# A graph layer and a mixture of experts: sums that end in PSUM in alternating banks, and a new order around expert 1

## The chip, the cores and the metric

The kernel runs on one core of one Trainium2 chip. The metric is the time of one execution on the device in microseconds (us), lower is better. Engines are named as in the profile: PE is TensorE's matrix multiplication, PEld its weight load, DVE is VectorE, ACT is ScalarE, POOL is GpSimd, SP is SyncE.

## What is computed

Two layers over 2048 rows of 256 numbers. The first is a graph layer with a 2048 x 2048 adjacency matrix, the second a feed-forward layer with 8 experts, of which each row takes the one with the highest logit, and a shared expert for all rows.

```python
deg = jnp.maximum((adj != 0).astype(jnp.float32).sum(-1), 1.0)[..., None]
h = layernorm(x)
dinv = rsqrt(deg)
pooled = (dinv * (adj + eye) * dinv) @ h + h
x = x + relu(pooled @ W + b)

xf = layernorm(x)
logits = xf @ gate_w.T                      # 8 experts
wts, idx = top_k(logits, 1); wts = softmax(wts)
h = silu(xf @ w1[e].T) * (xf @ w3[e].T)     # e: the row's expert, 1024 inner columns
y = (h * comb) @ w2[e].T
y = y + gelu(xf @ sw1.T) @ sw2.T            # the shared expert
x = x + y
```

## The kernel before

Every fp32 product is made from high and low parts: ACT rounds a tensor to its high part, DVE or POOL subtracts it from the original for the low part, and PE multiplies high by high, high by low and low by high in fp32r. The 2048 rows are 16 tiles of 128, and four tiles are a quarter (NQ = 4, QT = 4).

**The front.** For each tile t, z = layernorm(x) @ W is computed (`z_tile`), and its high and low parts are kept side by side in `zz`. Beside it the neighbour sums of quarter 0 run. **A quarter q** of neighbour sums (`agg_quarter`) multiplies 16 adjacency tiles (`agg_part`: `a_hi` from ACT, `a_lo` from POOL, line 395) by `zz` into four PSUM banks, one for each of the quarter's four row tiles; the left half of a bank holds the sum with z's high part, the right half that with its low part. `agg_end` adds the identity's share and closes the sums. The adjacency comes in chunks of two tiles into four buffers; SP loads the next one into a buffer when POOL has made its low parts and DVE has counted its nonzeros (`count_chunk`, lines 756 and 759). After the last count, `degrees` (line 1098) sums the counts by a matrix product.

DVE then ends the layer for the quarter: ACT copies the left halves to `agg` in SBUF (line 574), DVE adds the right halves (`sum_halves`, line 812), takes the inverse degree (`inverse_degree`), multiplies by it and adds z + bias (line 821), applies ReLU and adds to `resid` (line 825), both in `finish_gnn`.

**Shared blocks.** The layer norm of quarter q-1, its transposes (`xf_transposes`, into banks 4 and 5, or 0 and 1 in the last quarter) and their high and low parts (`xfT_highs`, `xfT_lows`) are made while quarter q is summed; behind the sums PE runs the gate of quarter q-1 and then `shared`: a row of 16 blocks (32 in the last run, which does quarters 2 and 3), each with `shared_up` (six products, line 1172), a GELU and its high part on ACT, the low part on POOL (line 411), and `shared_down` (four products, lines 1192 and 1194) two blocks later. The order within is written out by hand: a table of places says between which blocks `gate_back` (the gate's result transposed back), `ranks` (each row's rank in its expert) and, in the last run, the transposes, gate and ranks of quarter 3 stand. On ACT, `tanh_of_z` stands behind the first four GELUs of a quarter's blocks; it waits for `z_top_ok`, the last instruction of DVE's `choose`, and `choose` works on what `gate_back` leaves in PSUM. `shared_up` m waits until GELU m-2 has read its bank. POOL scatters a quarter's rows to `sorted_x` by expert, once `place_rows` has their places.

**Steps.** 23 steps of 128 sorted rows follow; with these inputs the experts need 2, 2, 2, 3, 2, 3, 3 and 3 steps by the reference's routing. A step does `up` (24 products, line 1253), a transpose of the next rows, `down` of the step before (lines 1280 and 1281) and `hid_transposes` (line 1266). Expert weights lie in `ering`, which has two slots. Each expert comes twice: as three high parts (1, 3 and 2 thousand columns, `expert_high`, POOL's own DMA queue, line 424), and as 12 raw pieces `eraw` of 512 columns through a ring of four buffers on SP's queue (line 338), from which POOL makes the 12 low parts (`expert`, line 445; DVE makes the first eight of expert 0). Low part 0 needs the first high part, low 2 the second, low 8 the third. A step's `up` waits for the first 8 low parts of its expert, its `down` for all 12. A slot's first two high parts are loaded when the expert in it has begun its last step's transposes (a wait on `xsT_ps` at low 8 of the expert before), the third when that expert's last `down` is done (a wait on `steps_done` at low 4). SP issues the first three row loads of `sorted_x` behind raw piece 11, and stores 16 tiles of `resid` between later raw pieces.

## Time and profile before

| | |
|---|---|
| three runs | 497.62, 493.37, 496.64 us, median 496.64 us |
| profiled execution, its own time | 496.5 us |
| its span, mean granted clock | 494.9 us, 0.976 |
| busy: PE / DVE / ACT / POOL | 91% / 55% / 40% / 67% of the span |
| DMA | 82.61 MB, mean 167 GB/s |

The span runs from the first to the last instruction of the core. A timeline row gives the start, the duration, the engine, the line and what it writes and reads; a bracket at its end gives the idle time of the engine before it and what ended that. "x4" joins four instructions in one row. A clock of 1.00 is 2.4 GHz for TensorE and 0.50 is 1.2 GHz.

### The profile page before, as it was taken

How to read it: one execution, taken by the hardware profiler on the slowest of the kernel's cores; microseconds unless marked ns; L12 is line 12 of the kernel's file. 1: busy time of each engine (PE TensorE's matmuls, PEld its weight loads, DVE VectorE, ACT ScalarE, POOL GpSimd, SP SyncE). 2: the span in 40 equal slices, each digit the busy share in tenths (PEclk: the TensorE clock that was granted, in tenths of full speed). 3: DMA queues.
4: the chain of work that ended last, by engine and by line, in shares of the span. 5: the costliest groups of instructions: out<-in, count | busy, mean ns of one | idle time of the engine just before them, and what ended most of it. 6: DMA issues, size and time to landing. Idle time of an engine off the chain costs nothing.

```text
span 494.9 us, 8933 instructions
## 1 busy us (share of the span) xinstructions
PE 449.6 (91%) x2620; PEld 384.3 (78%) x2621; DVE 272.4 (55%) x543; ACT 198.6 (40%) x435; POOL 333.0 (67%) x309
## 2 busy tenths in 40 slices
PE   5899977899989999889987999799999999999992
PEld 5788755798769887777975888688888888888881
DVE  4998799844687268858763334223343343333331
ACT  3655822564536543584552232222232332332330
POOL 3888857277955797557865675766667777888112
PEclk9999999999999999899999999889999999999997
DMA  7564240501341052369565689888888787455100
GB/s 250 190 210 156 79 149 22 182 1 49 122 153 61 2 176 98 81 225 357 145 199 171 229 280 331 250 315 281 324 279 301 254 307 234 59 70 73 11 1 0
DMA packets 41116, 82.61 MB, mean 167 GB/s; under 512 B 5120, under 2 KB 16768, under 8 KB 39040
## 3 DMA queue, kind: packets, MB, share of 16 engines
q1 hardware_dynamic: 28528, 47.60, 30.2%
q0 software_dynamic: 7536, 29.39, 19.0%
q10 hardware_dynamic: 5024, 5.27, 3.4%
q8 instruction: 15, 0.25, 0.2%
q14 instruction: 13, 0.11, 0.1%
HBM read 74.74 MB, written 8.41 MB: 168 GB/s over the span
## 4 chain that ended last, share of the span: by engine, by line
PE 50%; DVE 12%; POOL 10%; DMA 6%; issue 5%; ACT 3%; POOLq 1%; SPq 1%; DVEq 0%; ACTq 0%
PE bank L1253 20%; PE bank L1172 7%; PE bank L1280 7%; PE bank L1192 5%; DVE count L759 5%; POOL ering L445 4%; DMA eraw<-in_experts 4%; PE bank L1281 3%; POOL a_lo L395 3%; PE bank L1266 3%; DVE rows L735 3%; PE bank L1194 2%; DMA ering<-in_experts 1%; POOL gel_lo L411 1%; PE bank L1080 1%
## 5 line engine op out<-in xcount | busy, mean ns | idle before, releaser
L445 POOL TENSOR_TENSOR ering<-eraw,ering 128x512 fp32r<-128x512 f32 x88 | 111.9, 1307 | 54.2 <-DMA eraw<-in_experts 25.2
L1253 PE MATMUL bank<-ering,xsT_hi 128*128 x368 | 122.4, 404 | 6.1 <-POOL ering L445 3.4
L395 POOL TENSOR_TENSOR a_lo<-araw,a_hi 128x512 fp32r<-128x512 f32 x64 | 92.8, 1467 | 30.6 <-ACT a_hi L539 30.3
L1080 PE MATMUL bank<-zz,a_hi 128*128 128x512 f32 (+1 forms) x256 | 93.4, 405 | 7.1 <-POOL a_lo L395 7.0
L1000 DVE SCALAR_TENSOR_TENSOR hid<-bank,xs,sil 128x512 f32<-128x512 f32 x46 | 34.5, 751 | 98.7 <-ACT sil L663 98.7
L1253 PEld LDWEIGHTS bank<-ering,xsT_hi 128*128 128x128 f32 x368 | 70.4, 191 | 21.7 <-issue 6.6
L1253 PE MATMUL bank<-ering,xsT_lo 128*128 x184 | 72.7, 395 | 0.0
L1082 PE MATMUL bank<-zz,a_lo 128*128 128x256 f32 (+1 forms) x256 | 72.2, 282 | 0.0
L663 ACT ACTIVATE sil<-bank 128x512 f32<-128x512 f32 x46 | 27.5, 599 | 106.0 <-PE bank L1253 106.0
L1280 PE MATMUL bank<-ering,hidT_hi 128*128 x184 | 67.4, 406 | 1.2 <-DVE hidT_lo L1008 1.2
L411 POOL TENSOR_TENSOR gel_lo<-gel,gel_hi 128x256 fp32r<-128x256 f32 x58 | 43.9, 759 | 35.4 <-ACT gel_hi L597 34.5
L1080 PEld LDWEIGHTS bank<-zz,a_hi 128*128 128x128 f32 x256 | 48.7, 190 | 20.3 <-issue 8.6
L504 POOL DMA_INDIRECT out<-y_rows,row_token x23 | 35.9, 1559 | 31.5 <-DVE y_rows L1016 26.4
L539 ACT ACTIVATE a_hi<-araw 128x512 fp32r<-128x512 f32 x64 | 39.7, 628 | 34.7 <-PE bank L1082 23.1
L1192 PE MATMUL bank<-sw_r,gel_hi 128*128 128x512 f32 x128 | 48.9, 403 | 4.6 <-POOL gel_lo L411 3.0
L1281 PE MATMUL bank<-ering,hidT_lo 128*128 x184 | 51.5, 280 | 0.0
L1082 PEld LDWEIGHTS bank<-zz,a_lo 128*128 128x128 f32 x256 | 49.0, 191 | 0.0
L759 DVE SCALAR_TENSOR_TENSOR count<-araw,count 128x1024 bf16<-128x1024 f32 x28 | 45.8, 1635 | 2.8 <-DVE count L759 0.5
L1172 PE MATMUL bank<-xfT_hi,sw_hi 128*128 128x256 f32 x128 | 38.0, 297 | 4.2 <-DVE dinv L806 3.1
L1280 PEld LDWEIGHTS bank<-ering,hidT_hi 128*128 128x128 f32 x184 | 34.6, 188 | 8.6 <-issue 1.4
L1253 PEld LDWEIGHTS bank<-ering,xsT_lo 128*128 128x128 f32 x184 | 35.3, 192 | 7.0
L1172 PE MATMUL bank<-xfT_lo,sw_hi 128*128 128x256 f32 x128 | 36.5, 285 | 0.0
(154 smaller groups left out, 795.4 us busy)
## 6 DMA issues: line engine op xcount, KB each, us to landing
eraw<-in_experts SPq DMA_DIRECT2D x96, 256.0 KB, 5.5
araw<-in_adj_t SPq DMA_DIRECT2D x32, 512.0 KB, 4.7
ering<-in_experts POOLq DMA_DIRECT2D x8, 1536.0 KB, 8.5
ering<-in_experts POOLq DMA_DIRECT2D x8, 1024.0 KB, 7.7
ering<-in_experts POOLq DMA_DIRECT2D x8, 512.0 KB, 4.6
xs<-sorted_x ACTq DMA_DIRECT2D x20, 129.0 KB, 3.8
resid<-in_x SPq DMA_DIRECT2D x4, 512.0 KB, 9.0
sw_raw<-in_sw_t ACTq DMA_DIRECT2D x2, 1024.0 KB, 6.6
```

Of the source, the lines that this page charges most:

```text
L395: pool.tensor_tensor(a_lo[:, u % AR, :], araw[:, u // CJ, u % CJ, :], a_hi[:, u % AR, :].bitcast(F32), ALU.subtract).then_inc(adj_lo_ok, 1)
L411: pool.tensor_tensor(gel_lo[:, u, :], gel[:, u, :], gel_hi[:, u, :].bitcast(F32), ALU.subtract).then_inc(sh_lo, 1)
L445: pool.tensor_tensor(ering[:, slot, 1, c * ECW:(c + 1) * ECW], eraw[:, c % ER, :], ering[:, slot, 0, c * ECW:(c + 1) * ECW].bitcast(F32), ...
L539: act.activation(a_hi[:, u % AR, :], araw[:, u // CJ, u % CJ, :], ACT.Copy).then_inc(adj_hi_ok, 1)
L759: dve.scalar_tensor_tensor(into, araw[:, r, :, :], 0.0, into, ALU.not_equal, ALU.add).then_inc(adj_counted, CJ)
L1080: pe.matmul(acc(it)[:, :], a_hi[:, s, it * P:(it + 1) * P], zt, start=first, stop=False)
L1082: ins = pe.matmul(acc(it)[:, 0:D], a_lo[:, s, it * P:(it + 1) * P], zt[:, 0:D], start=False, stop=False)
L1172: ins = pe.matmul(bank[4 + m % 2][:, 0:HALF], w[:, k, ib * P:(ib + 1) * P], a[:, q % 2, k, half * HALF:(half + 1) * HALF], start=n == 0, s ...
L1192: pe.matmul(shared_bank(hq, k)[:, :], gel_hi[:, m % 2, k * P:(k + 1) * P], sw2_r[:, ib, :, :].rearrange("p h d -> p (h d)"), start=ib == 0 ...
L1253: ins = pe.matmul(bank[2 * w + h][:, :], a[:, k, :], ering[:, bass.ds(slot, 1), part, at:at + BANK].rearrange("p a n -> p (a n)"), start=n ...
L1280: pe.matmul(bank[6][:, :], hidT_hi[:, k, :], w2, start=k == 0, stop=False)
L1281: ins = pe.matmul(bank[6][:, 0:D], hidT_lo[:, k, :], ering[:, bass.ds(slot, 1), 0, W2AT + k * D:W2AT + (k + 1) * D].rearrange("p a n -> p ...
```

## The change

1. *Banks.* The four banks of the neighbour sums alternate: 0 to 3 in quarters 0 and 2, 4 to 7 in quarters 1 and 3. All that uses the other four (`xf_bank`, `gate_bank`, `logit_in`, `rank_in`, `degree_in`, `up_bank`, `shared_bank`) moves with them, with new waits for them.
2. *End of the layer.* `sum_halves` goes. `first_products` computes low half * dinv + (z + bias) in place in PSUM, `finish_gnn` adds high half * dinv to it in PSUM, and the ReLU and the addition to `resid` read PSUM. Twelve instructions per quarter stand where twelve stood.
3. *Order of DVE.* Two of the last four counts stand before `xfT_lows`, the inverse degree before the sums, the gate's copy between the products; in quarters 1 to 3 `choose` follows the end of the layer.
4. *Order of PE.* `degrees` stands before `agg_end`. `gate_back` is at place 6 of the shared blocks (5 in the last run) instead of 2, the ranks at 9 (7) instead of 5 (9). The wait for the last shared addition stands behind the `up` of step 1.
5. *Experts.* Expert 1's low parts wait for expert 0 at low 11 instead of low 8; for later experts the wait for `steps_done` and the third high part's load stand at low 3 instead of 4, and the next expert's first loads at low 9, behind low 8 as before. The three first row loads stand behind raw pieces 13, 14 and 15.

```diff
-    EARLY_RANKS_AT, STD_AT, THIRD_RANKS_AT, XF_AT, GATE_AT, RANKS_AT = 5, 8, 9, 10, 13, 16
+    EARLY_RANKS_AT, STD_AT, THIRD_RANKS_AT, XF_AT, GATE_AT, RANKS_AT = 9, 8, 7, 10, 13, 16
...
+        def acc(q, it):
+            return bank[(4 if q % 2 else 0) + it]
+        def other(q):
+            return 0 if q % 2 else 4
         def xf_bank(q, b):
-            return bank[(0 if q == NQ - 1 else 4) + b]
+            return bank[other(q + 1) + b]
...
                     sp.dma_start(eraw[:, c % ER, :], experts[e, :, c * ECW:(c + 1) * ECW]
                                  ).then_inc(eraw_loaded[c % ER], 16)
-                    if n == EC - 1:
+                    if n == EC + 1:
                         sp.wait_ge(routed, 1)
                         sp.wait_ge(scattered, 16 * NT)
                         sp.wait_ge(filled, 16 * (E + 1))
-                        for i in range(FIRST_ROWS):
+                    if EC + 1 <= n < EC + 1 + FIRST_ROWS:
+                        for i in range(n - EC - 1, n - EC):
...
+            def expert(e, slot, last=None, ahead=None, next_at=EC - 3):
+                for c in range(EC):
+                    static = isinstance(e, int)
+                    if c == EC // 4 and last is not None:
                         pool.wait_ge(steps_done, last)
+                        if static:
+                            low(e, slot, c)
+                        expert_high(e, slot, 2)
+                        if static:
+                            continue
+                    if c == next_at and ahead is not None:
                         pool.wait_ge(xsT_ps, ahead)
+                        if static:
+                            low(e, slot, c)
                         expert_high(e + 1, 1 - slot, 0)
                         expert_high(e + 1, 1 - slot, 1)
+                        if static:
+                            continue
+                    low(e, slot, c)
...
-            expert(1, 1, ahead=end_of(0))
+            expert(1, 1, ahead=end_of(0), next_at=EC - 1)
...
-            def sum_halves(q):
-                for it in range(QT):
-                    dve.wait_ge(agg_copied, q * QT + it + 1)
-                    dve.tensor_tensor(agg[:, it, :], acc(it)[:, D:2 * D], agg[:, it, :], ALU.add
-                                      ).then_inc(agg_free, 1)
-            def finish_gnn(q):
-                dve.wait_ge(agg_free, (q + 1) * QT)
+            def first_products(q):
                 dve.wait_ge(dinv_ok, q + 1)
                 dve.wait_ge(bias_added, (q + 1) * QT)
                 for it, t in enumerate(group(q)):
-                    chained(dve.scalar_tensor_tensor(agg[:, it, :], agg[:, it, :], dinv2[:, it:it + 1],
-                                                     norm[:, t, :], ALU.mult, ALU.add))
+                    dve.wait_ge(agg_copied, q * QT + it + 1)
+                    low = acc(q, it)[:, D:2 * D]
+                    chained(dve.scalar_tensor_tensor(low, low, dinv2[:, it:it + 1], norm[:, t, :], ALU.mult, ALU.add))
+            def finish_gnn(q):
+                settle()
+                for it in range(QT):
+                    low = acc(q, it)[:, D:2 * D]
+                    chained(dve.scalar_tensor_tensor(low, agg[:, it, :], dinv2[:, it:it + 1], low,
+                                                     ALU.mult, ALU.add))
                 settle()
                 for it, t in enumerate(group(q)):
-                    chained(dve.scalar_tensor_tensor(resid[:, t, :], agg[:, it, :], 0.0, resid[:, t, :],
-                                                     ALU.max, ALU.add))
-                settle()
+                    dve.scalar_tensor_tensor(resid[:, t, :], acc(q, it)[:, D:2 * D], 0.0, resid[:, t, :],
+                                             ALU.max, ALU.add).then_inc(agg_free, 1)
+                dve.wait_ge(agg_free, (q + 1) * QT)
...
                 normalize(NQ + q - 1, group(q - 1))
+                count_chunks(q, RAW, NC - 2)
                 xfT_lows(q - 1)
-                count_chunks(q, RAW, NC)
-                sum_halves(q)
+                count_chunks(q, NC - 2, NC)
+                inverse_degree(q)
+                first_products(q)
                 copy_gate(q - 1)
-                inverse_degree(q)
+                finish_gnn(q)
                 logits(q - 1)
                 if q < NQ - 1:
                     choose(q - 1)
-                finish_gnn(q)
-                if q < NQ - 1:
+                    read_ranks(q - 1)
                     place_rows(q - 1)
...
             hids(0, 0)
             rows_low(2, 1)
+            hid_lows(0)
             add_shared(2 * NQ - 1)
-            hid_lows(0)
...
                 for j in range(TURN, NT):
-                    agg_part(j, j % AR, q * NT + j)
+                    agg_part(q, j, j % AR, q * NT + j)
+                pe.wait_ge(xfT_lo_ok, 2 * q)
+                if q > 1:
+                    pe.wait_ge(sh_free, 4 * (q - 1))
+                degrees(q)
                 agg_end(q)
...
             def gate_back(q):
                 pe.wait_ge(gate_copied, q + 1)
+                pe.wait_ge(agg_free, min(q + 2, NQ) * QT)
...
-                degrees(q)
                 if q < NQ - 1:
-                    shared((q - 1) * 2 * NI, 2 * NI, {1: degrees_read(q), 2: lambda: gate_back(q - 1), EARLY_RANKS_AT: lambda: ranks(q - 1)})
+                    shared((q - 1) * 2 * NI, 2 * NI, {6: lambda: gate_back(q - 1), EARLY_RANKS_AT: lambda: ranks(q - 1)})
-            shared(LAST, 4 * NI, {1: degrees_read(NQ - 1), 2: lambda: gate_back(NQ - 2), THIRD_RANKS_AT: lambda: ranks(NQ - 2),
+            shared(LAST, 4 * NI, {5: lambda: gate_back(NQ - 2), THIRD_RANKS_AT: lambda: ranks(NQ - 2),
...
-            pe.wait_ge(sh_free, 2 * 2 * NQ)
             def one_step(s, u, loads):
                 up(s)
+                if u == 1:
+                    pe.wait_ge(sh_free, 2 * 2 * NQ)
```

The program's rows below name line, operation, output<-inputs, shape and the semaphores that a row waits for. Line numbers of the changed kernel are its own: 1123 and 1125 are `agg_part`, 1132 `agg_end`, 1141 `degrees`, 1197 the gate, 1207 `gate_back`, 1221 `shared_up`, 1243 and 1245 `shared_down`, 460 the experts' low parts, 444 their high parts' loads.

On PE, the end of a quarter's sums, before (1080 and 1082 are `agg_part`, 1089 `agg_end`, 1151 the gate, 1098 `degrees`, 1172 `shared_up`):

```order
L1080 MATMUL bank<-zz,a_hi 128x512
L1082 MATMUL bank<-zz,a_lo 128x256
L1089 MATMUL bank<-zz,ident_r 128x512 x4
L1151 MATMUL bank<-xfT_hi,gate_r 16x512 [waits xfT_lo_ok,split_lo]
L1151 MATMUL bank<-xfT_lo,gate_r 16x512
L1151 MATMUL bank<-xfT_hi,gate_r 16x512
L1151 MATMUL bank<-xfT_lo,gate_r 16x512
L1098 MATMUL bank<-ones,count 128x1 [waits adj_counted]
L1098 MATMUL bank<-ones,count 128x1 x7
L1172 MATMUL bank<-xfT_hi,sw_hi 128x256
```

The same place in the changed kernel:

```order
L1123 MATMUL bank<-zz,a_hi 128x512
L1125 MATMUL bank<-zz,a_lo 128x256
L1141 MATMUL bank<-ones,count 128x1 [waits adj_counted,xfT_lo_ok]
L1141 MATMUL bank<-ones,count 128x1 x7
L1132 MATMUL bank<-zz,ident_r 128x512 x4
L1197 MATMUL bank<-xfT_hi,gate_r 16x512 [waits xfT_lo_ok,split_lo]
L1197 MATMUL bank<-xfT_lo,gate_r 16x512
L1197 MATMUL bank<-xfT_hi,gate_r 16x512
L1197 MATMUL bank<-xfT_lo,gate_r 16x512
L1221 MATMUL bank<-xfT_hi,sw_hi 128x256
```

The degree's eight matmuls, and with them the wait for the last count, moved from behind the gate to in front of `agg_end`.

On PE, around the gate's transposes in the shared blocks of quarter 1, before (1160 is `gate_back`, 1192 and 1194 `shared_down`):

```order
L1172 MATMUL bank<-xfT_hi,sw_lo 128x256
L1160 MATMUL bank<-ident,gate_out 128x16 [waits gate_copied]
L1160 MATMUL bank<-ident,gate_out 128x16 x3
L1172 MATMUL bank<-xfT_hi,sw_hi 128x256 [waits sh_gelu]
L1172 MATMUL bank<-xfT_lo,sw_hi 128x256
L1172 MATMUL bank<-xfT_hi,sw_lo 128x256
L1172 MATMUL bank<-xfT_hi,sw_hi 128x256
L1172 MATMUL bank<-xfT_lo,sw_hi 128x256
L1172 MATMUL bank<-xfT_hi,sw_lo 128x256
L1192 MATMUL bank<-sw_r,gel_hi 128x512 [waits sh_lo,agg_free]
```

In the changed kernel:

```order
L1243 MATMUL bank<-sw_r,gel_hi 128x512
L1245 MATMUL bank<-sw_r,gel_lo 128x256
L1207 MATMUL bank<-ident,gate_out 128x16 [waits agg_free,gate_copied]
L1207 MATMUL bank<-ident,gate_out 128x16 x3
L1221 MATMUL bank<-xfT_hi,sw_hi 128x256 [waits sh_gelu]
L1221 MATMUL bank<-xfT_lo,sw_hi 128x256
L1221 MATMUL bank<-xfT_hi,sw_lo 128x256
L1221 MATMUL bank<-xfT_hi,sw_hi 128x256
L1221 MATMUL bank<-xfT_lo,sw_hi 128x256
L1221 MATMUL bank<-xfT_hi,sw_lo 128x256
L1243 MATMUL bank<-sw_r,gel_hi 128x512 [waits sh_lo]
```

The transposes stood before the third up block (m = 2, which waits for GELU 0); now they stand before the seventh (m = 6, which waits for GELU 4).

On POOL, the last low parts of expert 1 and the loads for expert 2, before:

```order
L445 TENSOR_TENSOR ering<-eraw,ering 128x512 [waits eraw_loaded3]
L445 TENSOR_TENSOR ering<-eraw,ering 128x512 [waits eraw_loaded0,ehi_loaded2,xsT_ps]
L424 DMA ering<-in_experts 128x1024
L424 DMA ering<-in_experts 128x3072
L445 TENSOR_TENSOR ering<-eraw,ering 128x512 [waits eraw_loaded1]
L445 TENSOR_TENSOR ering<-eraw,ering 128x512 [waits eraw_loaded2]
L445 TENSOR_TENSOR ering<-eraw,ering 128x512 [waits eraw_loaded3]
```

In the changed kernel:

```order
L460 TENSOR_TENSOR ering<-eraw,ering 128x512 [waits eraw_loaded0,ehi_loaded2]
L460 TENSOR_TENSOR ering<-eraw,ering 128x512 [waits eraw_loaded1]
L460 TENSOR_TENSOR ering<-eraw,ering 128x512 [waits eraw_loaded2]
L460 TENSOR_TENSOR ering<-eraw,ering 128x512 [waits eraw_loaded3,xsT_ps]
L444 DMA ering<-in_experts 128x1024
L444 DMA ering<-in_experts 128x3072
```

The wait for `xsT_ps` and the two loads behind it moved from low 8 to low 11.

## Rows read from the trace of the kernel before

**Rows 1.** The page, part 1: busy us of each engine, share of the span.
```profile
PE 449.6 (91%) x2620; PEld 384.3 (78%) x2621; DVE 272.4 (55%) x543; ACT 198.6 (40%) x435; POOL 333.0 (67%) x309
```

**Rows 2.** The chain that ended last, steps 6 to 8: start us, us, what.
```profile
319.10 8.35 PE bank L1253 x24
...
331.37 5.51 PE bank L1253 x24
...
340.80 5.51 PE bank L1253 x24
```

**Rows 3.** TensorE's timeline: start, us, engine, line, operation, out<-in, count, idle before.
```profile
71.04 0.49 PE L1080 MATMUL bank<-zz,a_hi 128*128 x1 [3.25 <-POOL a_lo L395]
...
94.10 0.42 PE L1160 MATMUL bank<-ident,gate_out 16*128 16x16 f32 x4
...
142.62 1.09 PE L1089 MATMUL bank<-zz,ident_r 128*128 128x512 f32 x4
...
144.86 0.35 PE L1098 MATMUL bank<-ones,count 128*128 128x1 bf16 x8 [0.23 <-DVE count L759]
...
149.12 0.39 PE L1192 MATMUL bank<-sw_r,gel_hi 128*128 128x512 f32 x1
...
150.53 0.39 PE L1192 MATMUL bank<-sw_r,gel_hi 128*128 128x512 f32 x1
...
218.09 0.39 PE L1172 MATMUL bank<-xfT_hi,sw_hi 128*128 128x256 f32 x1 [1.14 <-ACT gel L593]
...
268.34 0.49 PE L1253 MATMUL bank<-ering,xsT_hi 128*128 x1 [2.72 <-issue]
...
319.10 0.79 PE L1253 MATMUL bank<-ering,xsT_hi 128*128 x1 [3.38 <-POOL ering L445]
```

**Rows 4.** VectorE's timeline: the end of quarter 0, the choice, quarters 1 and 2, step 0.
```profile
54.96 1.42 DVE L812 TENSOR_TENSOR agg<-bank,agg 128x256 f32<-128x256 f32 x4 [2.48 <-ACT agg L574]
...
59.49 3.62 DVE L825 SCALAR_TENSOR_TENSOR resid<-agg,resid 128x256 f32<-128x256 f32 x4
...
96.70 0.15 DVE L885 TENSOR_TENSOR weight<-top 128x4 f32<-128x4 f32 x1
...
97.10 2.32 DVE L821 SCALAR_TENSOR_TENSOR agg<-agg,dinv,rows 128x256 f32<-128x256 f32 x4 [0.24 <-issue]
...
137.79 0.69 DVE L832 TENSOR_TENSOR xfT_lo<-bank,xfT_hi 128x512 fp32r<-128x512 f32 x1 [0.56 <-ACT xfT_hi L584]
...
138.40 6.41 DVE L759 SCALAR_TENSOR_TENSOR count<-araw,count 128x1024 bf16<-128x1024 f32 x4
...
265.61 0.75 DVE L861 TENSOR_TENSOR resid<-bank,resid 128x256 f32<-128x256 f32 x2
```

**Rows 5.** ScalarE's timeline: tanh and GELU in quarter 1, copies of quarter 2.
```profile
97.94 0.19 ACT L579 ACTIVATE weight<-weight 128x4 f32<-128x4 f32 x1
...
98.37 0.39 ACT L593 ACTIVATE gel<-bank 128x256 f32<-128x256 f32 x1 [0.24 <-PE bank L1172]
...
143.74 1.21 ACT L574 ACTIVATE agg<-bank 128x256 f32<-128x256 f32 x4 [5.46 <-PE bank L1089]
```

**Rows 6.** POOL's timeline: a low part of GELU, then the experts' low parts.
```profile
147.27 0.73 POOL L411 TENSOR_TENSOR gel_lo<-gel,gel_hi 128x256 fp32r<-128x256 f32 x1 [1.62 <-ACT gel_hi L597]
...
274.42 1.30 POOL L445 TENSOR_TENSOR ering<-eraw,ering 128x512 fp32r<-128x512 f32 x1 [7.47 <-PE bank L1042]
...
290.45 0.57 POOL L424 DMA_DIRECT2D ering<-in_experts  x1
...
309.46 5.05 POOL L445 TENSOR_TENSOR ering<-eraw,ering 128x512 fp32r<-128x512 f32 x4 [4.04 <-DMA eraw<-in_experts]
```

**Rows 7.** Windows: busy us (instructions) per engine, granted clock, DMA share, GB/s.
```profile
202.00:203.00 1.00, 1.00 (x7) 0.77 (x6) 0.00 (x0) 0.32 (x1) 0.03 (x1) 0.50 0.00 0
...
267.00:268.00 1.00, 0.00 (x0) 0.00 (x0) 0.56 (x1) 0.00 (x0) 0.00 (x0) 1.00 0.79 220
```

**Rows 8.** SyncE's timeline: the first rows of expert 0.
```profile
250.66 2.53 SPq L346 DMA_DIRECT2D xs<-sorted_x  x3
```

145 lines of the change are left out of this document (79 added, 66 removed).

## The prediction

> **What bounds the kernel now.** I read the page's first part, then the chain that ended last, then each engine's timeline around the places where that chain changes engine. TensorE is busy 91% of a span of 494.9 us [rows 1], so the reader should look for the holes in the other 9%, and for stretches at the half clock. From 331 us on the chain is TensorE alone: the 24 up products of a step take 5.51 us, and a step 9.43 us, from 331.37 to 340.80 [rows 2]. No edit touches those steps, so the whole question lies before 331 us. The largest hole is at step 6, the first of expert 3: TensorE waits 3.38 us for POOL's low parts of expert 3 and then needs 8.35 us where the next step needs 5.51 [rows 2, 3]: 2.84 us of half clock on top of the wait. A smaller hole, 2.72 us, stands before step 1 [rows 3]. In front of the steps lie the four quarters of the neighbour sums. There TensorE's holes are short, as the 0.23 us at 144.86, except 3.25 us in quarter 1 [rows 3].
>
> **The change, part by part.** The sum is made against the profiled execution: 496.5 us, span 494.9 and 1.6 around it. The median of the runs shown is 496.64, so the two may stand for each other.
>
> *The end of the layer in PSUM, quarter 0.* Now VectorE takes from 54.96 to 63.11 us, 8.15 us, for four sums of halves (1.42), the degree, four products and four ReLU additions (3.62 from 59.49) [rows 4]. Products and additions read and write SBUF only, and POOL subtracts beside them; the same four products take 2.32 us in quarter 1 [rows 4]. Everything VectorE does in quarter 1 is one chain behind this, and the adjacency loads hang on its counts: that is the 3.25 us hole. The changed kernel has twelve instructions for these twelve, but each has one operand in PSUM. The nearest rows are the sums of halves, 1.42 us for four, 0.35 each, and at the other end the undisturbed SBUF products, 2.32 for four, 0.58 each. I take 0.40 to 0.45, some 5.2 us with two settles, and the degree is already done when the sums come; but the sums come 0.35 us later, because the degree matmuls now stand before them. 8.15 - 5.2 - 0.35 = 2.6 us earlier. With 0.58 each it is about 1, and if contention goes on nothing; with 0.35 it is 3.7. Term: **-2.6** (0 to -3.7).
>
> A rule speaks against this part. The Trainium skill, "VectorE: DVE Perf Modes", section "Rules for kernel authors", says that for elementwise work on matmul output one may copy PSUM to SBUF first if many operations follow. Its errata section prices a VectorE operation at 58 cycles and the elements from SBUF and at 120 from PSUM, at 0.96 GHz; by that the twelve would cost 12 x 0.065 = 0.8 us more, and the sum would be 0.8 us higher. The rows say the reverse for this kernel, 1.42 us for four from PSUM against 2.32 from SBUF, so I go by the rows.
>
> *Two counts ahead of the low parts of xfT, quarters 1 to 3.* VectorE's second xfT_lo now waits 0.56 us for ACT, and the four counts (6.41 us) begin behind it [rows 4]. With two counts in front, the wait is covered: the last count ends 0.6 us earlier per quarter. Term: **-1.7** (0 to -2).
>
> *The degree moves in front of the quarter's last four matmuls.* Before, TensorE closes the sums and runs the gate while VectorE still counts, then waits 0.23 us for the counts and starts the degree at 144.86; its first down product (L1192) follows at 149.12, 4.26 us later [rows 3]. Beside that, ACT begins the copies of the sums at 143.74, and POOL has the first low part ready at 148.00, 4.26 us later as well [rows 5, 6]; it is done before TensorE asks for it. Now the closing matmuls, and so ACT's copies, stand behind the counts: degree 0.35, close 1.09 [rows 3], then those 4.26 us and hand-overs, 5.8 us. So 1.5 us more in quarters 1 and 2. In quarter 3 the clock is at half in that stretch already [rows 7], so that TensorE's own path is the longer one, and I take 0.2 more there. What was hidden, ACT's copies and table load, loses its cover. Term: **+3.2** (0 to +5).
>
> *The gate's transposes go from place 2 to place 6 of the shared blocks.* This is the most expensive edit. On ACT the tanh of a quarter stands, as before, behind the fourth GELU, and it waits for the last instruction of `choose`. Now that is timely: transposes at 94.10, last instruction of `choose` from 96.70 to 96.85, tanh at 97.94, so 1.1 us to spare [rows 3 to 5]. In the changed order TensorE issues the transposes after four blocks, and the very next instruction, `shared_up` 6, waits for GELU 4, which is behind that tanh on ACT. Queued behind it on TensorE are all later blocks; POOL's gel_lo waits as well. The round trip is 2.75 us to the end of choose, 0.2 for the tanh, 0.4 for the GELU [rows 5] and 0.15 of hand-overs, 3.5 us, of which the transposes themselves fill 0.4: 3.1 us of hole, once each for quarters 1 and 2. Nothing else is on TensorE's queue to fill it. Below it could be 0 if the tanh is not reached in time; above it is 3.5. Term: **+6.2** (0 to +7).
>
> *Last run of shared blocks.* Transposes at place 5 and ranks at 7 instead of 2 and 9. Between eight GELUs and the ninth ACT loads three tables, and TensorE has a hole of 1.14 us there [rows 3]; before, ranks and transposes were done beside that or earlier, now both lie in front of the eighth GELU: 0.4 for the transposes and as much for the ranks. Term: **+0.9** (0 to +1.8).
>
> *Clock.* A hole of 3.25 us in quarter 1 and one of 3.38 at step 6 each brought a stretch at 1.2 GHz; so did a thin stretch at 201 us (clock 0.50 from 202), while the 2.72 us before step 1 brought none (1.00 from 267 to 268) [rows 2, 3, 7]. Two new holes of 3.1 us lie between these. The stretch behind step 6's hole cost 2.84 us, and it was the longest; I take 1.7, and count one of the two. Term: **+1.7** (0 to +5).
>
> *Order at step 0 and 1.* VectorE's last addition of the shared result (0.75 us at 265.61) [rows 4] releases TensorE's queue at 266.4, and step 1 starts 1.9 us later, by what stands there the time of two register loads. The wait now stands behind step 1's up products, so the loads can begin when the transposes are issued, 1.35 us sooner: **-1.35** (0 to -1.5). The first row of x is issued behind raw piece 13 instead of at 250.66 [rows 8], 1.5 to 2 us later, and its transpose was due some 2 us after it had landed: **+0.3** (0 to +1.5).
>
> *Expert 1's lows run through.* Now POOL waits 7.47 us before low 8 of expert 1 for the end of expert 0 (at 274.42). Behind it come the high parts of expert 2 and waits for raw pieces, as 4.04 us at 309.46; the third high part of expert 2 is issued at 290.45, and low 7 of expert 3 ends just before 319.1 [rows 3, 6]. With the wait moved to low 11, three raw pieces of expert 2 are loaded before the high parts, and the third high part goes out at piece 3 instead of 4, as soon as expert 0's last down product is done. That is some 8.7 us into step 2: 268.3 - 1.35 + 9.43 + 8.7 = 285.1, 5 us before the present issue. At expert 3 the same place is two steps on, 304.0; low 3 then ends at 305.3 and low 7 at 305.3 + 4 x 1.30 = 310.5 us. Step 6 is due at 266.9 + 5 x 9.43 = 314. So POOL is some 3 us ahead instead of 3.4 behind. Wait and half clock go: **-6.2** (0 to -6.2). Next late is nothing: expert 3 has three steps, 28 us for 24 us of POOL.
>
> Sum: -2.6 - 1.7 + 3.2 + 6.2 + 0.9 + 1.7 - 1.35 + 0.3 - 6.2 = +0.45. 496.5 + 0.5 = **497.0 us**. The gain at the experts is paid back by the shared blocks.
>
> **Rivals.** *The round trip costs nothing* (0.22). If the tanh does not hold TensorE, both holes and their clock go: 497.0 - 6.2 - 1.7 = 489.1 us. For it: today's 1.1 us to spare; against it: the transposes move by four blocks, and a block is 1.41 us, from 149.12 to 150.53 [rows 3].
>
> *Slower: step 6 stays late* (0.12). One mechanism: raw pieces and high parts share the DMA engines, and the wait at 309.46 is for a raw piece [rows 6]. If the loads only bunch up, expert 3's low 7 comes after 314 + 3 us, the hole and the half clock stay, and 497.0 + 6.2 = 503.2 us. It decides from the moment that low 7 of expert 3 ends later than about 314 us; between 314 and 316 it would cost only that time.
>
> *Slower: the clock falls at each weak place* (0.08), the second new hole and two quarter ends as well: + 3 x 1.7 = 502.1 us. For it: the thin stretch at 201 [rows 7]; against it: the other two quarter ends kept their clock.
>
> *The change doesn't do what it says* (0.04): POOL's run is held by the raw pieces in quarter 0 to 1 as before, and VectorE gains nothing; about 500.
>
> **How the numbers follow.** Forecast 0.54, with its own range 493.5 to 500.5. A measurement of this kernel can tell about 1%, 5 us, from no change. Faster by more: nearly all of the first rival and a tail of the forecast, 0.23. Slower by more: the second, half of the third and a tail, 0.20. Within: 0.57. The range from 490.5 to 502.5 leaves out about half of the first and of the second rival.
>
> **What would show each step.** Right: in quarters 1 and 2 one TensorE hole of about 3 us before the seventh up product of the shared blocks, with ACT waiting for the tanh's input; a hole of 1.5 us before the degree matmuls; the hole at 71 us shrunk; VectorE's first quarter end near 60.5 us; POOL's lows of expert 1 in one run to the eleventh; no wait before step 6 and 5.5 us for its up products; step 1 some 1.9 us behind the last transposes' issue. The prediction is wrong if the seventh up product follows without a hole (then near 489), or if step 6 still waits (then near 503).

## The result, and the profile after

The changed kernel takes 506.29 us (median of 4 executions, 503.85 to 508.96) against 497.13 for the kernel before, a ratio of 1.019 with an interval of 1.015 to 1.024: slower by 1.9%. The forecast was 497.0 and its range ended at 502.5. The profiled execution took 506.04 us, its span is 504.5.

TensorE's timeline of the changed kernel, read against [rows 3]:

```profile
89.23 0.34 PE L1141 MATMUL bank<-ones,count 128*128 128x1 bf16 x8 [2.14 <-DVE count L793]
89.43 1.19 PE L1132 MATMUL bank<-zz,ident_r 128*128 128x512 f32 x4
...
95.43 0.47 PE L1243 MATMUL bank<-sw_r,gel_hi 128*128 128x512 f32 x1 [0.23 <-POOL gel_lo L431]
...
100.51 0.42 PE L1207 MATMUL bank<-ident,gate_out 16*128 16x16 f32 x4
...
103.96 0.48 PE L1221 MATMUL bank<-xfT_hi,sw_hi 128*128 128x256 f32 x1 [3.03 <-ACT gel L626]
...
162.25 0.58 PE L1221 MATMUL bank<-xfT_hi,sw_hi 128*128 128x256 f32 x1 [2.62 <-ACT gel L626]
...
276.50 0.49 PE L1300 MATMUL bank<-ering,xsT_hi 128*128 x1 [1.36 <-POOL ering L460]
...
328.70 0.79 PE L1300 MATMUL bank<-ering,xsT_hi 128*128 x1 [4.80 <-POOL ering L460]
```

The forecast round trip is there: 3.03 and 2.62 us in front of the seventh up block (L1221), right behind the gate's transposes (L1207). The hole before step 1 halved, from 2.72 to 1.36. But step 6, where a hole of 3.38 us and a stretch at half clock should have gone, now waits 4.80.

ScalarE, where [rows 5] had the tanh without a wait:

```profile
103.26 0.20 ACT L612 ACTIVATE weight<-weight 128x4 f32<-128x4 f32 x1 [4.97 <-DVE weight L920]
103.53 0.38 ACT L626 ACTIVATE gel<-bank 128x256 f32<-128x256 f32 x1
```

ACT sits 4.97 us in front of the tanh, and the GELU that TensorE waits for stands behind it.

Windows of TensorE behind its holes (columns as in [rows 7]; the last three are clock, DMA share and GB/s):

```profile
88.00:92.00 4.00, 2.77 (x16) 1.69 (x17) 2.24 (x6) 1.32 (x5) 0.00 (x0) 0.81 0.69 212
92.00:96.00 4.00, 3.77 (x22) 3.46 (x22) 3.97 (x11) 3.36 (x7) 1.29 (x2) 0.77 0.41 142
...
104.00:108.00 4.00, 4.00 (x18) 3.76 (x19) 0.00 (x0) 1.85 (x5) 1.98 (x3) 0.57 0.00 0
...
160.00:164.00 4.00, 1.75 (x7) 1.75 (x8) 1.35 (x8) 1.69 (x5) 1.27 (x2) 0.77 0.00 0
164.00:168.00 4.00, 4.00 (x24) 3.58 (x23) 0.00 (x0) 2.28 (x6) 1.52 (x3) 0.81 0.00 0
```

The clock falls behind both round trips, and at the end of quarter 1 as well, where the kernel before had kept it.

VectorE's quarter 0 and the counts of quarter 1, against [rows 4], and POOL beside them:

```profile
55.63 1.67 DVE L849 SCALAR_TENSOR_TENSOR bank<-bank,dinv,rows 128x256 f32<-128x256 f32 x4 [1.20 <-ACT agg L607]
57.33 1.67 DVE L856 SCALAR_TENSOR_TENSOR bank<-agg,dinv,bank 128x256 f32<-128x256 f32 x4
59.03 1.42 DVE L860 SCALAR_TENSOR_TENSOR resid<-bank,resid 128x256 f32<-128x256 f32 x4
...
80.87 4.53 DVE L793 SCALAR_TENSOR_TENSOR count<-araw,count 128x1024 bf16<-128x1024 f32 x2
...
86.52 2.57 DVE L793 SCALAR_TENSOR_TENSOR count<-araw,count 128x1024 bf16<-128x1024 f32 x2
```

```profile
60.60 21.49 POOL L415 TENSOR_TENSOR a_lo<-araw,a_hi 128x512 fp32r<-128x512 f32 x11 [2.38 <-ACT a_hi L572]
```

VectorE is done with quarter 0 at 60.45 instead of 63.11, 2.66 us earlier, as forecast. But POOL then makes eleven low parts without a wait for data, 1.95 us each, and two counts beside it take 4.53 us where the next two take 2.57. The last count ends at 89.09, 1.85 us earlier than before; the degree now stands in front of the close, TensorE waits 2.14 us for it, and the first down product comes at 95.43, 0.2 us later than before.

POOL's low parts of experts 2 and 3, against [rows 6]:

```profile
282.58 1.30 POOL L460 TENSOR_TENSOR ering<-eraw,ering 128x512 fp32r<-128x512 f32 x1 [5.17 <-PE bank L1084]
283.81 1.15 POOL L444 DMA_DIRECT2D ering<-in_experts  x2
288.97 2.54 POOL L460 TENSOR_TENSOR ering<-eraw,ering 128x512 fp32r<-128x512 f32 x2 [4.01 <-DMA ering<-in_experts]
...
295.39 0.57 POOL L444 DMA_DIRECT2D ering<-in_experts  x1 [1.34 <-PE bank L1328]
...
303.08 2.51 POOL L460 TENSOR_TENSOR ering<-eraw,ering 128x512 fp32r<-128x512 f32 x2 [2.04 <-DMA eraw<-in_experts]
...
312.34 1.29 POOL L460 TENSOR_TENSOR ering<-eraw,ering 128x512 fp32r<-128x512 f32 x1 [1.91 <-DMA ering<-in_experts]
316.56 2.56 POOL L460 TENSOR_TENSOR ering<-eraw,ering 128x512 fp32r<-128x512 f32 x2 [2.92 <-DMA eraw<-in_experts]
319.05 0.56 POOL L444 DMA_DIRECT2D ering<-in_experts  x1
319.63 3.79 POOL L460 TENSOR_TENSOR ering<-eraw,ering 128x512 fp32r<-128x512 f32 x3
325.87 3.71 POOL L460 TENSOR_TENSOR ering<-eraw,ering 128x512 fp32r<-128x512 f32 x3 [2.46 <-DMA eraw<-in_experts]
```

Low 11 of expert 1 waits 5.17 us for the same event as low 8 did before. Then comes a wait that the forecast had not counted: 4.01 us until the first high part of expert 2 has landed. The third high part of expert 2 goes out at 295.39 and that of expert 3 at 319.05, 23.66 us later, with three more waits for loads between them. And behind the third high part of expert 3 (319.05) stand lows 3 to 7, with 2.46 us of wait for raw piece 6 among them.

### The profile page after: what moved, and what is told of

Read it like the earlier page. It is cut to its first block, busy times and chain, and to the rows that moved or that the text cites. A ratio compares the mean times of both kernels' runs of the same rounds, so it can differ in the third digit from the quotient of the medians.

```text
span 504.5 us, 8940 instructions
## 1 busy us (share of the span) xinstructions
PE 453.9 (90%) x2620; PEld 387.5 (77%) x2621; DVE 269.8 (53%) x543; ACT 198.7 (39%) x435; POOL 337.1 (67%) x309
## 4 chain that ended last, share of the span: by engine, by line
PE 54%; POOL 17%; issue 8%; DVE 8%; DMA 6%; ACT 4%; SPq 2%; POOLq 0%; ACTq 0%; DVEq 0%
PE bank L1300 21%; POOL a_lo L415 9%; PE bank L1327 7%; DMA eraw<-in_experts 5%; PE bank L1221 5%; POOL ering L460 4%; PE bank L1243 4%; PE bank L1328 4%; PE bank L1313 3%; PE bank L1123 3%; DVE rows L769 2%; PE bank L1245 2%; PE bank L1107 2%; PE bank L1125 2%; PE bank L1084 1%
## 5 line engine op out<-in xcount | busy, mean ns | idle before, releaser
L415 POOL TENSOR_TENSOR a_lo<-araw,a_hi 128x512 fp32r<-128x512 f32 x64 | 98.2, 1554 | 25.4 <-ACT a_hi L572 25.2
L1221 PE MATMUL bank<-xfT_hi,sw_hi 128*128 128x256 f32 x128 | 38.5, 301 | 8.3 <-ACT gel L626 8.3
L1221 PE MATMUL bank<-xfT_lo,sw_hi 128*128 128x256 f32 x128 | 37.2, 291 | 0.0
```

Of the source, the lines that this page charges most:

```text
L415: pool.tensor_tensor(a_lo[:, u % AR, :], araw[:, u // CJ, u % CJ, :], a_hi[:, u % AR, :].bitcast(F32), ALU.subtract).then_inc(adj_lo_ok, 1)
L1221: ins = pe.matmul(up_bank(m)[:, 0:HALF], w[:, k, ib * P:(ib + 1) * P], a[:, q % 2, k, half * HALF:(half + 1) * HALF], start=n == 0, stop=n ...
```

## Where the time went, by place

The start of four landmarks in each trace, us: the first down product of quarters 1, 2 and 3, the transpose of step 0's rows, the first up product of steps 1 and 6, and the span. The experiments of the next section are in it already. Each row is one execution: those of tanh_late and third_high_later are the fastest of their runs (495.45 and 500.56 us against medians of 497.98 and 502.33), that of best_ranks9 is the slowest of its run (489.70 against 488.43). Single traces differ by more than a microsecond even where no edit reaches: experts_alone, whose edit concerns experts 1 and later, has its quarter 2 down product at 150.59, 1.5 us behind the kernel before.

| kernel | down q1 | down q2 | down q3 | rows 0 | step 1 | step 6 | span |
|---|---|---|---|---|---|---|---|
| before | 95.25 | 149.12 | 204.47 | 254.84 | 268.34 | 319.10 | 494.9 |
| changed | 95.43 | 154.13 | 212.28 | 264.02 | 276.50 | 328.70 | 504.5 |
| tanh_late | 95.03 | 149.03 | 203.02 | 254.03 | 267.06 | 319.16 | 493.9 |
| close_first | 93.42 | 151.97 | 210.00 | 261.19 | 273.74 | 327.28 | 502.7 |
| experts_back | 95.63 | 154.84 | 213.51 | 264.46 | 276.56 | 327.60 | 502.6 |
| third_high_later | 95.54 | 154.20 | 212.37 | 263.46 | 276.21 | 325.16 | 499.0 |
| best_ranks9 | 92.34 | 145.72 | 198.98 | 249.54 | 262.40 | 313.36 | 488.1 |

So the changed kernel is +0.2 at quarter 1's end, +5.0 and +7.8 behind the next two, +9.2 at the first rows, +8.2 at step 1 and +9.6 from step 6 on. Most of it, 7.8, is there at quarter 3's down product, where the terms of the forecast add up to 6.8; what was forecast to give it back, step 6, adds 1.4.

## The experiments

**tanh_late.** The round trip taken away:

```diff
                 if q < NQ - 1:
-                    shared_blocks((q - 1) * 2 * NI, NI // 2)
+                    shared_blocks((q - 1) * 2 * NI, NI)
                     tanh_of_z(q - 1)
-                    shared_blocks((q - 1) * 2 * NI + NI // 2, NI // 2)
```

> The changed kernel with one edit: in quarters 1 and 2 ACT runs the tanh of the gate behind the eighth GELU of the shared blocks instead of the fourth. Theory A (the loss lies in front of the experts; half of it is the round trip that starts with the gate's transposes at place 6 and is waited for by the tanh, 3.03 us at 103.96 and 2.62 at 162.25, with stretches at half clock behind both): both holes are under 0.5 us, the clock is 1.00 behind them, the row transpose of step 0 comes 6 to 8.5 us earlier than 264.0 and the total is 498 to 500.5 us. Theory B (the holes are covered by something else that is late next, such as the ranks at place 9, which need the same choose): the holes move to the ranks, 2 us each, and the total is 502 to 505 us. Theory C (the end is set by POOL's stream of low parts, which starts from the end of expert 0 only loosely): the front gains but step 6 waits 4.8 us plus what was gained, and the total stays at 505 to 506.

Measured: 497.98 us (10 executions), ratio 1.001 (0.999 to 1.004) against 1.019. On TensorE the transposes stay where they were and no hole follows in quarter 1 or 2:

```profile
100.11 0.42 PE L1206 MATMUL bank<-ident,gate_out 16*128 16x16 f32 x4
...
154.11 0.42 PE L1206 MATMUL bank<-ident,gate_out 16*128 16x16 f32 x4
```

and the tanh follows its GELU at once:

```profile
103.62 0.42 ACT L630 ACTIVATE gel_hi<-gel 128x256 fp32r<-128x256 f32 x1 [0.29 <-PE bank L1244]
103.94 0.19 ACT L612 ACTIVATE weight<-weight 128x4 f32<-128x4 f32 x1
```

Theory A. The round trip and its clock are worth 8.3 us by the medians; two holes are 5.65 of it.

**close_first.** The degree back behind close and gate:

```diff
-                pe.wait_ge(xfT_lo_ok, 2 * q)
-                if q > 1:
-                    pe.wait_ge(sh_free, 4 * (q - 1))
-                degrees(q)
                 agg_end(q)
+                pe.wait_ge(xfT_lo_ok, 2 * q)
+                if q > 1:
+                    pe.wait_ge(sh_free, 4 * (q - 1))
...
                 gate(q - 1)
+                degrees(q)
```

> The changed kernel with one edit: TensorE closes the sums (four matmuls with the identity) and runs the gate before it waits for VectorE's counts and takes the degree, in quarters 1 to 3, as the kernel before did. Theory A (degree in front of the close costs 1.5 to 2 us a quarter, since ACT's copies of the sums and its table load hang behind it; 5.8 us from degree to first down product against 4.3 before): the first down product of quarters 2 and 3 comes 3 to 5 us earlier than 154.13 and 212.28, the total is 501.5 to 503.5 us. Theory B (the counts are now as early as the close, TensorE waits only 0.18 us for them in quarters 2 and 3, so that the order of the two matters little, under 0.4 us a quarter): the total is 505 to 506.5.

Measured: 504.39 us, ratio 1.019 (1.012 to 1.025): by the times not to be told from the changed kernel. The trace says more. At the end of quarter 1 TensorE's wait for the counts falls from 2.14 to 0.22 us, and the clock stays at 1.00 from 88 to 96 us:

```profile
90.11 0.35 PE L1141 MATMUL bank<-ones,count 128*128 128x1 bf16 x8 [0.22 <-DVE count L793]
...
93.42 0.47 PE L1242 MATMUL bank<-sw_r,gel_hi 128*128 128x512 f32 x1 [0.39 <-POOL gel_lo L431]
```

Down products come 2.0, 2.2 and 2.3 us earlier: nearly all of the gain is in quarter 1, and quarters 2 and 3, where theory A put it, add little. Step 1's hole is followed by half clock here, so that step 2 comes 10.98 us behind step 1 and not 9.41 as in the changed kernel; that takes back 1.6. Both theories had the place wrong: the order matters where VectorE is late with the counts, in quarter 1. (With the tanh late as well, quarters 2 and 3 add 0.7 us each: from one down product to the next it is 54.0 us in tanh_late and 53.3 in tanh_close_h2.)

**experts_back** and **experts_alone.** The expert part undone in the changed kernel, and done alone in the kernel before:

```diff
-                    if n == EC + 1:
+                    if n == EC - 1:
...
-            expert(1, 1, ahead=end_of(0), next_at=EC - 1)
+            expert(1, 1, ahead=end_of(0))
...
-                    if c == EC // 4 and last is not None:
+                    if c * ECW == EP[2] // 2 and last is not None:
```

> The changed kernel with the whole edit of the expert part undone: POOL waits for the end of expert 0 before low 8 of expert 1 and takes the third high part behind low 4, and SP issues the first three rows of x together behind raw piece 11. Theory A (the run-through gives nothing: high parts of expert 2 can only be issued once expert 0's rows are through, 19.8 us behind the row transpose of step 0 against 20.8 before, and from there DMA sets 22 to 24 us per expert): step 6 still waits 3 to 5 us and the total is 505 to 507. Theory B (the run-through harms step 6: two more lows stand behind the third high part, whose 1 MB goes ahead of raw pieces 6 and 7): step 6's wait falls to 3.4 us or below, total 503.5 to 505. Theory C (the run-through works as forecast but is masked by the front): total 508 to 512.

> The kernel before with the expert part of the change alone (POOL's run-through of expert 1, third high part ahead of low 3, rows of x one at a time behind raw pieces 13 to 15). My prediction on record would make it 6 us faster, 490.5. Theory A (nothing gained, since the stream starts from the end of expert 0 and DMA sets its rate): 496 to 498, with step 6 waiting 3 to 5 us. Theory B (it harms step 6 by 1.4 us and the first rows arrive 1 us late): 498 to 499.5.

Measured: undone 503.03 us, ratio 1.014 (1.007 to 1.022); alone 500.38, ratio 1.010 (1.006 to 1.013). By the medians the expert part costs 3.3 us in the one place and 3.9 in the other; the second is clear of 1. Step 6's hole is 2.10 us without it and 4.97 with it alone. Theory A (gives nothing) falls, theory B (it harms) stands; both totals lie outside its bands, by 0.5 us below and by 0.9 above. In the trace of experts_alone 1.6 us are clock behind step 1, which theory B did not count.

**third_high_later.** Of the expert part, only the third high part put back behind low 4:

```diff
-                    if c == EC // 4 and last is not None:
+                    if c == EC // 3 and last is not None:
                         pool.wait_ge(steps_done, last)
-                        if static:
-                            low(e, slot, c)
+                        low(e, slot, c)
                         expert_high(e, slot, 2)
-                        if static:
-                            continue
+                        continue
```

> The changed kernel with one edit: POOL issues the third high part of each expert behind low 4, as the kernel before did, and no longer in front of low 3; the run-through of expert 1 and SP's rows stay. Over the kernels so far, step 6 starts 44.6 to 45.0 us after the first high part of expert 2 is issued where the expert edit is in, 42.1 and 43.4 where it is not. Theory A (the third high part's 1 MB, issued two lows earlier, goes ahead of raw pieces 6 and 7 of expert 3, which step 6 needs): that distance falls to 42 to 43.4 us, the wait at step 6 to 2 to 3.4 us, the total to 502.5 to 504.5 us. Theory B (the loss comes from the run-through itself or from SP's order): the distance stays above 44.5 and the total at 505.5 to 506.5.

Measured: 502.33 us, ratio 1.011 (1.008 to 1.014), which is clear of the changed kernel's 1.019 and slightly under theory A's 502.5. POOL's timeline around the third high part of expert 3, and TensorE's step 6:

```profile
315.46 5.05 POOL L460 TENSOR_TENSOR ering<-eraw,ering 128x512 fp32r<-128x512 f32 x4 [3.02 <-DMA eraw<-in_experts]
320.46 0.57 POOL L444 DMA_DIRECT2D ering<-in_experts  x1
321.04 3.77 POOL L460 TENSOR_TENSOR ering<-eraw,ering 128x512 fp32r<-128x512 f32 x3
```

```profile
325.16 0.50 PE L1298 MATMUL bank<-ering,xsT_hi 128*128 x1 [1.37 <-POOL ering L460]
```

Lows 5 to 7 follow without a wait. The distance from the issue of expert 2's first high part to step 6 is 41.6 us; it is 44.9 in the changed kernel. Distance and hole are under theory A's bands too (42 and 2 us). Theory A: by the medians the third high part in front of low 3 is the expert part's whole loss, 4.0 us against 3.3 for undoing all of it. In this trace 2.0 us of the gain are clock: step 7 comes 9.42 us behind step 6, against 11.43 in the changed kernel.

**stores_later.** SP's stores out of the way:

```diff
-    STORE_FROM = 2 * EC + ER
+    STORE_FROM = 4 * EC
```

> The changed kernel with one edit: SP's 16 stores of the shared result (128 KB each) start at raw piece 48 instead of 28, so that none stands between the raw pieces of experts 2 and 3. Theory A (the DMA engines' bytes set the rate of POOL's stream before step 6: about six stores, 0.8 MB, at 260 to 290 GB/s are 2.7 to 3 us): step 6's wait falls from 4.8 to about 2 us and the total to 503 to 504. Theory B (waits are for latency of single pieces and the stores fit beside them): under 1 us, total 505.3 to 506.5. In both, later steps may wait more, since the stores come then.

Measured: 505.91 us, ratio 1.021 (1.015 to 1.026). Theory B by the total. The trace lies between the theories: step 6's hole falls from 4.80 to 3.26 us, so the stores have a share in it. Step 6 starts 1.2 us earlier, but 0.7 of these are lost again behind it, and the median moves by 0.4.

**run_alone.** The kernel before with the run-through of expert 1 and SP's rows, third high part as it stood (the edit of experts_alone, and that of third_high_later upon it).

> The kernel before with the run-through of expert 1's low parts and SP's interleaved first rows, but the third high part behind low 4 as it stood. Theory A (the run-through only exchanges one wait for another: three lows of expert 1 no longer stand behind the first high part of expert 2, but POOL then waits 4.0 us for that high part to land and 1.2 for the second): the same as before within noise, 495.5 to 497.5, with the distance from the issue of expert 2's first high part to step 6 at 41.5 to 43.5 us. Theory B (it is worth something, since the kernel with only the third high part put back came to 502.3, slightly under the 503.0 of the kernel with the whole expert part undone): 494.5 to 495.5. Theory C (SP's rows between raw pieces delay step 0 or 1): 498 to 499.

Measured: 495.29 us, ratio 0.998 (0.995 to 1.002). POOL:

```profile
275.22 1.15 POOL L425 DMA_DIRECT2D ering<-in_experts  x2
280.17 2.55 POOL L441 TENSOR_TENSOR ering<-eraw,ering 128x512 fp32r<-128x512 f32 x2 [3.80 <-DMA ering<-in_experts]
284.25 3.78 POOL L441 TENSOR_TENSOR ering<-eraw,ering 128x512 fp32r<-128x512 f32 x3 [1.54 <-DMA ering<-in_experts]
287.97 0.57 POOL L425 DMA_DIRECT2D ering<-in_experts  x1
```

From the first high part's issue to the third's it is 12.75 us, against 14.8 in [rows 6] (275.66 to 290.45): three lows fewer, 3.8 us, but two waits, 5.3 us together, for high parts in their place, and a wait for a raw piece (3.60 us) less. To step 6 it is 41.8 us from the first issue, as theory A has it, against 43.4 before. The median, 0.9 us under the kernel before, lies in theory B's band; the interval covers both, and excludes more than 2.6 us of gain.

**counts_back.** All four counts behind the low parts of xfT, in the changed kernel:

```diff
-                count_chunks(q, RAW, NC - 2)
                 xfT_lows(q - 1)
-                count_chunks(q, NC - 2, NC)
+                count_chunks(q, RAW, NC)
```

> The changed kernel with one edit: VectorE takes all four last counts of a quarter behind the low parts of xfT again, in quarters 1 to 3. Theory A (two counts in front were worth what the trace shows, 8.2 us from rows to last count in the kernel before against 6.2 in quarters 2 and 3 of the changed one, and TensorE's degree waits for the last count): 1.5 to 2 us a quarter in quarters 2 and 3, less in quarter 1; total 509 to 511 us. My prediction priced it at 0.6 us a quarter: total 508. Theory B (the saved time is only idle time of VectorE, since the close waits for matmuls anyway): 506 to 507.

Measured: 510.95 us, ratio 1.029 (1.025 to 1.033): theory A, 4.7 us. TensorE's degree waits 2.27 and 2.63 us for the last count in quarters 2 and 3, where it waited 0.18.

**sbuf_end.** The end of the layer in VectorE's old form: four sums of halves into SBUF, four products and four additions on SBUF alone (the hunk of the products is left out here):

```diff
-                    low = acc(q, it)[:, D:2 * D]
-                    chained(dve.scalar_tensor_tensor(low, low, dinv2[:, it:it + 1], norm[:, t, :], ALU.mult, ALU.add))
+                    chained(dve.tensor_tensor(agg[:, it, :], acc(q, it)[:, D:2 * D], agg[:, it, :], ALU.add))
...
-                    dve.scalar_tensor_tensor(resid[:, t, :], acc(q, it)[:, D:2 * D], 0.0, resid[:, t, :],
+                    dve.scalar_tensor_tensor(resid[:, t, :], agg[:, it, :], 0.0, resid[:, t, :],
```

> The changed kernel with VectorE's arithmetic at the layer's end as the kernel before had it: sums of halves out of PSUM into SBUF, then four products and four ReLU additions on SBUF alone; order of the work and banks stay. Theory A (PSUM operands are quicker than SBUF ones beside a busy POOL, about 0.40 us each against 0.58 to 0.90; 2.66 us in quarter 0, of which 1.85 reached the end of quarter 1's counts): VectorE's quarter 0 ends near 62.5 instead of 60.45, row transpose of step 0 comes 1 to 3 us later than 264.0, total 507 to 509. Theory B (in quarter 1 POOL's eleven low parts of adjacency, 1.95 us each, set the time whatever VectorE does first): total 505.5 to 506.8, end of quarter 1's counts within 0.5 us of 89.09.

Measured: 511.22 us (506.86 to 514.67), ratio 1.026 (1.015 to 1.036). VectorE's quarter 0:

```profile
56.96 2.66 DVE L854 SCALAR_TENSOR_TENSOR agg<-agg,dinv,rows 128x256 f32<-128x256 f32 x4
59.65 2.51 DVE L858 SCALAR_TENSOR_TENSOR resid<-agg,resid 128x256 f32<-128x256 f32 x4
```

It ends at 62.16, and 1.7 of the 2.66 us are gone. Quarter 1's counts end at 88.87, no later than with PSUM, and the down product of quarter 1 comes at 95.28, as theory B says. The total goes with theory A and beyond its 509, with a wide interval. In the trace 2.2 us are lost between the down products of quarters 1 and 2, and the first rows come 3.6 us later. One part of it is POOL: its first low part behind quarter 2's sums takes 1.16 us instead of 0.73 beside VectorE's products and additions on SBUF, and TensorE waits 0.81 us for it instead of 0.38.

**tanh_close_h2**, **tanh_close_exback**, **best_ranks9.** tanh_late and close_first together with third_high_later, or with experts_back; and the first of these with the ranks of the last run at place 9:

```diff
-    EARLY_RANKS_AT, STD_AT, THIRD_RANKS_AT, XF_AT, GATE_AT, RANKS_AT = 9, 8, 7, 10, 13, 16
+    EARLY_RANKS_AT, STD_AT, THIRD_RANKS_AT, XF_AT, GATE_AT, RANKS_AT = 9, 8, 9, 10, 13, 16
```

> The changed kernel with three edits together: the tanh behind the eighth GELU, sums closed and gate run ahead of the degree, third high part behind low 4. If the effects add (measured so far: 8.3 us for the tanh, 1.9 for the close), 496.1 less 2 to 3 for the third high part: 493 to 494.5 us, faster than the kernel before by 0.4 to 0.7%. If an earlier front only makes step 6 wait longer for POOL's stream: 495.5 to 496.5.

> Tanh behind the eighth GELU, sums closed ahead of the degree, and the whole expert part as before. Against the kernel with these two and only the third high part put back (489.3) it tells what the run-through is worth in this place. Theory A (nothing, as in the kernel before): 488.8 to 490. Theory B (it is worth 0.7 us or more, as the pair 502.3 and 503.0 hints): 490 to 491.5.

> The three edits that made 489.3 (tanh late, close ahead of the degree, third high part behind low 4), and in the last run of shared blocks the ranks at place 9 instead of 7. Theory A (as forecast, the ranks at 7 stand in front of the eighth GELU and cost 0.4 us, and at 9 they are done beside ACT's table loads): 488.5 to 489.2. Theory B (the row positions behind the ranks are then late for the next transposes): 489.5 to 491.

Measured: 489.32 us, ratio 0.984 (0.981 to 0.987); 490.57, ratio 0.990 (0.983 to 0.997); 488.43, ratio 0.983 (0.976 to 0.990). All three beat both kernels. The first is 3.7 us faster than the 493 that addition gives. The first is 17 us under the changed kernel, where the single edits had given 8.3, 1.9 and 4.0, together 14.2. What the run-through and the ranks' place add (1.3 and 0.9 us by the medians) is within the spread.

**counts_alone**, **close_counts**, **best_sbuf.** Three crossings, to see whether an edit's worth is its own: the counts' order alone in the kernel before; close_first with counts_back; and best_ranks9 with sbuf_end.

> The kernel before with one edit of the change alone: two of VectorE's four last counts of a quarter stand ahead of the low parts of xfT. My prediction on record priced it at -1.7 us, 494.9. Theory A (in the order before, close and gate stand in front of the degree, and TensorE waits only 0.23 us for the counts, so that earlier counts have almost nothing to give): 495.5 to 496.7. Theory B (the 4.6 us that it is worth in the changed kernel are worth as much here): 491.5 to 493.

> The changed kernel with two edits: sums closed and gate run ahead of the degree, and all four last counts behind the low parts of xfT. Theory A (the two edits act on one wait: with the close first, late counts are covered by close and gate, 2.4 us of TensorE): 505 to 506.5, so counts are worth 1 to 2 us here and not 4.6. Theory B (additive, 504.4 + 4.6): 508.5 to 509.5.

> The kernel with the four edits (488.4: tanh late, close first, third high part behind low 4, ranks of the last run at 9) with VectorE's arithmetic at the layer's end on SBUF as the kernel before had it. Theory A (its worth was 4.9 us in the changed kernel because products and additions stood in the chain to the gate's transposes, whose round trip ACT and TensorE waited for; with the tanh late that chain is slack, and only quarter 0's 1.8 us can count, of which none reached the end of quarter 1's counts, 88.87 against 89.09): 488.3 to 489.7. Theory B (worth the same everywhere): 492.5 to 494.

Measured: 494.68 us, ratio 0.996 (0.994 to 0.997); 503.56, ratio 1.013 (1.010 to 1.016); 498.03, ratio 1.002 (1.000 to 1.005). The counts' order is worth 2.2 us in the kernel before, between the two theories. With the close first it is worth nothing in the changed one: 503.56 without it, 504.39 with it, where it was worth 4.7 with the degree in front. So counts and close act on one wait. The PSUM arithmetic is worth 9.6 us in the best kernel, which neither theory had. Windows of best_sbuf and then of best_ranks9 show where a good part of it lies, quarter 1:

```profile
70.00:74.00 4.00, 3.25 (x11) 2.79 (x12) 3.97 (x9) 1.44 (x4) 4.00 (x4) 0.63 0.75 219
...
82.00:86.00 4.00, 3.60 (x13) 3.19 (x14) 3.87 (x6) 1.48 (x3) 1.45 (x2) 0.50 0.14 46
86.00:90.00 4.00, 4.00 (x19) 3.46 (x18) 2.71 (x3) 0.00 (x0) 0.30 (x1) 0.74 0.90 289
...
98.00:102.00 4.00, 3.98 (x17) 3.66 (x18) 1.70 (x4) 1.10 (x3) 1.48 (x2) 0.57 0.02 4
```

```profile
84.00:88.00 4.00, 4.00 (x24) 3.22 (x23) 3.87 (x5) 0.07 (x1) 0.20 (x1) 1.00 0.62 202
88.00:92.00 4.00, 3.67 (x30) 2.60 (x28) 3.48 (x9) 3.91 (x10) 0.54 (x1) 1.00 0.69 219
```

With SBUF arithmetic TensorE loses its clock three times between 70 and 102 us and is 5.7 us late at quarter 1's first down product (98.03 against 92.34) and 8.7 at quarter 2's (154.42 against 145.72), though VectorE's counts of quarter 1 end at 88.84, as early as in best_ranks9 (88.97). A second part is POOL, at the end of every quarter. Its low part of the first GELU stands beside VectorE's products. The first two rows are best_sbuf, the third is best_ranks9:

```profile
95.71 2.17 POOL L431 TENSOR_TENSOR gel_lo<-gel,gel_hi 128x256 fp32r<-128x256 f32 x1 [9.41 <-ACT gel_hi L628]
98.03 0.50 PE L1237 MATMUL bank<-sw_r,gel_hi 128*128 128x512 f32 x1 [1.80 <-POOL gel_lo L431]
...
91.46 0.74 POOL L431 TENSOR_TENSOR gel_lo<-gel,gel_hi 128x256 fp32r<-128x256 f32 x1 [7.26 <-ACT gel_hi L628]
```

With the products on SBUF it takes 2.17 us instead of 0.74, and TensorE waits for it 1.8 us in each of quarters 1 to 3 instead of 0.4: 4.2 us of the 9.0 between the two spans. It is one execution of each; how the rest divides between clock and a later quarter 0 was not measured apart.

## Why the prediction was wrong

*The round trip of the gate's transposes* was right: place, size (forecast 2 x 3.1 us, measured 3.03 and 2.62) and worth (forecast 6.2 and 1.7 of clock, measured 8.3 by taking it away). The clock fell behind both holes, where I counted one.

*Expert 1's lows* is the step that failed, and it is most of the miss: forecast -6.2 at step 6, in the trace +1.4, 7.6 of the 9.0 us by which the profiled execution missed. The forecast had low 7 of expert 3 ready 3.5 us ahead of step 6 (310.5 against 314); it was 4.8 us late. These 8.3 us can be followed from step 1 on (forecast 266.9, measured 276.50).

The third high part of expert 2 was forecast 18.2 us behind step 1 and came 18.9 behind it: nearly right. The next line of the forecast, "at expert 3 the same place is two steps on, 304.0", is where most was lost. It lets POOL's stream go at the pace of TensorE's steps, 18.9 us for the two steps of expert 2. But from this load to the same load of expert 3 it is 23.66 us, and it was 24.0 in the kernel before (290.45 in [rows 6] to this row):

```profile
314.44 0.57 POOL L424 DMA_DIRECT2D ering<-in_experts  x1
```

Between the two stand 12 low parts, 15.2 us, 1.7 us of issuing loads, and the waits of 2.04, 1.91 and 2.92 us for raw pieces and a high part. So 4.8 us went here. The prediction itself had "24 us of POOL" for an expert, and held it against the 28 us of a three-step expert only.

The other places are smaller. First, "three raw pieces of expert 2 are loaded before the high parts" is true but gains little, 0.9 us by the median of run_alone and not clear of nothing. POOL's three lows had stood in the time in which the high part was on its way; taken away, POOL waits 4.01 us for it instead. Second, low 7 of expert 3 was reckoned as "305.3 + 4 x 1.30", POOL's own pace. With the third high part in front of low 3, raw piece 6 comes late (the wait of 2.46 us at 325.87), and low 7 ends 9.3 us behind the third high part's load instead of 6.5: the load that only `down` needs was put ahead of pieces that `up` needs. Putting it back gives 4.0 us. That the loads and not the steps set the pace is read from these waits; no run changed the loads' rate. The rival "step 6 stays late" had this result and nearly this mechanism, with 0.12; [rows 6] already showed POOL waiting 4.04 us for a raw piece in the middle of that stretch, which should have forbidden the sum at POOL's pace.

*The end of the layer in PSUM*: the size in quarter 0 was right (2.66 us on VectorE, forecast 2.6), and the pitch too (1.67, 1.67 and 1.42 us for four). One row behind it was misread: the 2.32 us for four SBUF products were not undisturbed, since POOL's gel_lo ran beside them (at 98.11, 1.02 us instead of 0.74). With POOL idle for most of their time they take 1.65 (sbuf_end, at 153.82), no more than the 1.67 out of PSUM. The gain is the contention that PSUM avoids, not a quicker source. That it reaches quarter 1's end was wrong: only 1.85 us reached the last count together with the reordering of counts, since VectorE and POOL slow each other there, and with the degree in front of the close none reached the first down product. That misses 1.9 us at quarter 1's end, forecast -1.7 and measured +0.2. The rule weighed in the prediction (the Trainium skill, "VectorE: DVE Perf Modes", errata) made PSUM operands the dearer. The traces do not agree: nearly undisturbed, four products take 1.67 us with PSUM and 1.65 without, and beside POOL in quarter 0 it is 1.67 against 2.66. Four ReLU additions take 1.42 us out of PSUM and 2.51 out of SBUF; there POOL stood idle beside the first (58.22 to 60.60) and ran beside the end of the second. The prediction also counted twelve dearer instructions, but the four sums of halves had read PSUM before.

*The counts*: forecast -1.7, measured 2.2 us in the kernel before. The number came by luck, not by the mechanism. The last count comes 2.0 us earlier in a quarter, not 0.6, since the four counts take 5.1 us instead of 6.4; but TensorE had waited only 0.23 us for them, and the trace of counts_alone is 0.3 us ahead at quarter 1's down product and 0.9 at quarter 2's. The other 2.1 at quarter 3's stand where the clock, 0.72 from 200 to 204 us in the kernel before, stays at 1.00. In the changed kernel they are worth 4.7, as they only make up for the degree's new place.

*The degree in front of the close*: forecast +3.2. The 5.8 us from degree to down product came as forecast (5.82 in quarters 2 and 3), but the close in it is no added time: it had stood in front of the degree before. The hole of 1.5 us before the degree was 2.14 in quarter 1 and 0.18 in the others. The undoing gave 1.9 by the medians, not clear of zero, 2.0 to 2.3 in the trace, nearly all of it in quarter 1.

*Last run of blocks, rows and step 1*: between quarter 3's first down product and the first rows the offset grew by 1.4 us (forecast 0.9 and 0.3), and fell by 1.0 to step 1 (forecast 1.35). Right in size, in one trace; no run took these edits apart.

What stays open: adding the single edits' effects in the changed kernel (8.3, 1.9 and 4.0 back, 4.7 and 4.9 lost) gives 4.6 of the 9.2 us between the medians. The crossings show that the terms are not their own: counts with close (4.7 or 0), the PSUM arithmetic with the rest (4.9 or 9.6). They don't divide the other 4.6. Not run at all were the alternating banks, the gate's transposes back at place 2 (tanh_late takes away what they cost, by another way) and the order at steps 0 and 1.

## What to carry to other kernels

Taking a queued item out of a transfer's way gains only if something else fills the transfer's time: before moving work ahead of a wait, look at what the wait behind it would be. A stream that waits for loads keeps the loads' pace: forecast its next station from the time it took last time, and not from the engine that starts it. A load that is needed later must not be issued in front of loads that are needed sooner, even if its buffer is free. And when two engines are coupled by a request and an answer, move both ends: the transposes went four blocks back, the tanh stayed, and one line on ACT was worth 8.3 us.

## What the runs showed of the hardware

The same short hole does not always cost the same. In all kernels with step 1's wait moved, TensorE has a hole of 1.33 to 1.38 us before step 1. Behind it step 2 comes 9.4 or 9.5 us later in the changed kernel, tanh_late, tanh_close_exback, third_high_later, stores_later, counts_back and best_sbuf, and 11.0 in close_first, tanh_close_h2, best_ranks9, experts_back, close_counts and sbuf_end. A hole of 2.7 us does no better at telling: 9.4 us in the kernel before and run_alone, 10.9 in counts_alone and 11.0 in experts_alone. There is one trace of each, so that it may be a matter of the execution and not of the kernel. The windows of close_first and of the changed kernel behind that hole:

```profile
274.00:278.00 4.00, 4.00 (x12) 3.10 (x12) 1.14 (x4) 0.00 (x0) 0.34 (x1) 0.57 0.60 178
```

```profile
276.00:280.00 4.00, 3.50 (x15) 2.92 (x16) 1.92 (x5) 0.44 (x1) 1.41 (x2) 1.00 0.79 233
```

The clock is 0.57, mostly the lower level, in the first, and 1.00 in the second. That is 1.6 us for a hole of one size, and it took back more than half of the 2.8 us by which close_first led at step 1.

VectorE and POOL slow each other where both read two tensors from SBUF: POOL's adjacency low part takes 1.95 us beside VectorE in quarter 1, an expert's low part of the same size beside a quieter VectorE 1.27 (5.07 for four), and two counts take 4.53 or 2.57 us. VectorE's instructions with one operand in PSUM don't show it: four products take 1.67 us beside POOL's adjacency low parts in quarter 0, where four on SBUF take 2.66, and four additions take 1.42 us in quarter 1 (at 95.03) beside POOL's gel_lo, which takes 0.74. In best_sbuf four products on SBUF take 1.65 us and POOL's gel_lo beside them 2.17; there it is POOL that is held up. The Trainium skill ("SBUF — State Buffer", section "SBUF: two separate sides") says that VectorE and GpSimd share a pair of ports, which a VectorE instruction with two SBUF inputs needs against a GpSimd instruction that reads SBUF, and that one blocks the other for a whole instruction. The rows here agree: where two such instructions meet, one or both take longer, and the 2.17 us are about the usual 0.74 and the rest of the products. It would have spoken for the PSUM arithmetic and against a free gain in quarter 1, where POOL runs without a break.
